# Laying out pixels for the values' stationaries in a small buffer, in a vision tower on one core

## The chip, the cores and the metric

The kernel runs on one core of one Trainium2 chip. The metric is the device time of one execution in microseconds; of several executions the median is taken.

## The reference

The input `x` is 128 images of 64 channels, 64 x 64 pixels, float32. Per image:

```python
x = features.reshape(b, c, h, s, w, s)              # windows of 4 x 4 pixels, s = 4
reduce_feats = x.mean((3, 5))...                    # one token per window: 256 tokens
unf = ...                                           # the 16 pixels of each window
q = _ln(reduce_feats) @ Wq.T                        # one query per window
kv = _ln(unf) @ Wkv.T                               # keys and values of 16 pixels
attn = softmax(einsum('bhpd,bhpnd->bhpn', q * scale, k))
aggre = einsum('bhpn,bhpnd->bhpd', attn, v)         # 8 heads
h = reduce_feats + aggre @ proj_w.T + proj_b
h = layernorm(h + lightning_attention(h))           # causal, with decay, chunks of 128
h = layernorm(h + moe(h))                           # 8 experts, top 2, gelu
```

The change concerns the values of the 16 pixels, `v`.

## The kernel before

Two blocks follow each other. The first (tokenizer and attention) works on 128 units; the second (experts) begins when it is done. A unit is one half (128 windows) of two images: 64 channels of one image lie on partitions 0 to 63, those of the other on 64 to 127, and the unit's 2048 pixels lie along the free dimension of one of the four buffers of `xb`. They stand in the order of the image: four pixel rows `b` of a window (512 floats each), in each the 128 windows `t`, in each window the four pixel columns `d`. SyncE loads a unit by four transfers (line 286) as soon as the unit four before has done its values (`v_pe`).

All engines run their own `step(i, r)`, written out by hand: unit 4i + r enters, and work on the units one to six before is interleaved with it, counted by semaphores. The steps of a loop iteration are four (r = 0 to 3); in every second one (s = 1) the attention's state is updated as well.

TensorE's order in a step is: `selected` (lines 317, 320: reduces keys and centred squares of the unit before), `attended` (455), `state` (462, s = 1), `keys(0)`, `attn_qk` (391, 392), `turned` (331, 332), `scores(0)` (412), `values(0)`, `keys(1)`, `attn_vk` (399), `values(1)`, `attend(0)` (427), `queries` (377), `keys(2)`, `scores(1)`, `values(2)`, `queries_turned` (385), `keys(3)`, `aggregated` (443), `values(3)`, `projected` (448), `attend(1)` (427, and 434 for s = 1). `keys_free(j)` ahead of `keys(j)` waits until VectorE and ScalarE have read the keys' two banks of the group before (`kq_done`, `cs_done`).

`keys(j)` (342, 347) multiplies the weights as stationary by the pixels of row j. `values(j)` (366) is the other way round: the pixels are the stationary, so that the windows come out on partitions. For pixel column j it takes, of each pixel row b, the pixels of 128 windows, which is every fourth float of `xb`, as one 128x128 stationary, and streams 128 columns of weights. Each fp32 product is issued as two passes, each with a weight load and a matmul; a group `values(j)` has 4 products and 8 passes. The result goes to the bank `VB`, and ScalarE copies it to `vs` (line 524).

ScalarE further squares the centred pixels (517), copies `oT` (529), `ssb` (533), `qT` and `kT` (542, 543), `vpad`, `vpl`, `kpl` and `htok` (555 to 563), takes over the queries (`qps`, 568), and begins the layer norms' inverse root (581 to 584). VectorE finishes it by a Newton step (818 to 820), scales the queries (825), forms key times query (`kqs`, 752), the softmax (835 to 858), the masks of the attention scores (763) and the reduction of values times weights (`agg`, 800). GpSimd multiplies values by weights (636, 643), and sums the pixels of the unit two ahead (666 to 674).

Of the kernel before, what the change touches and what calls it, by code (L numbers as in the profile page):

```python
# [6 lines left out]
ACT = mybir.ActivationFunctionType  # L7
# [6 lines left out]
def vit_tower_kernel(nc, x, ln_q_w, ln_q_b, Wq, ln_kv_w, ln_kv_b, Wkv, proj_w, proj_b,  # L14
                     w_qkv, w_proj, b_proj, slopes, router_w, w1, b1, w2, b2, out):
    P = 128
    B, C, HH, WW = x.shape
    ST = 4
# [17 lines left out]
    def done(i, r, lag, per, plus=0):  # L36

        if isinstance(i, int):
            return max(0, max(0, min(UNITS, 4 * i + r - lag + 1)) * per + plus)
        return i * (4 * per) + (r - lag + 1) * per + plus  # L40

    def there(i, r, lag):
        return not isinstance(i, int) or 0 <= 4 * i + r - lag < UNITS
# [20 lines left out]
    def units(eng, step):  # L64

        step(-1, 2)
        step(-1, 3)
        for i in (0, 1):
            for r in range(4):
                step(i, r)  # L70
        with eng.Fori(2, UNITS // 4 - 1) as i:
            for r in range(4):
                step(i, r)
        for u in range(UNITS - 4, UNITS + 6):
            step(u // 4, u % 4)

    with ExitStack() as ctx:
        def sb(name, shape, dt=F32):
            return ctx.enter_context(nc.sbuf_tensor(name, shape, dt))

        def sem(name):
            return ctx.enter_context(nc.semaphore(name))
# [6 lines left out]
        VB = ps[:, 2, :]  # L89
# [13 lines left out]
        w_ckv = sb("w_ckv", [P, 3 * P])  # L103
# [17 lines left out]
        with ExitStack() as early:  # L121
            def sb1(name, shape, dt=F32):
                return early.enter_context(nc.sbuf_tensor(name, shape, dt))
# [18 lines left out]

            xb = sb1("xb", [P, 4, PX])
            xt = sb1("xt", [P, PX // 2])
            l2 = sb1("l2", [P, P])
            vs = sb1("vs", [P, 2, N * P])
            kqs = sb1("kqs", [P, ST, PX // ST])
# [47 lines left out]
            x_in = [sem("x_in%d" % r) for r in range(4)]  # L195
            kc_pe = sem("kc_pe")
            kq_done = sem("kq_done")
            cs_done = sem("cs_done")
            v_pe = sem("v_pe")
            vs_done = sem("vs_done")  # L200
            sel_pe = sem("sel_pe")
# [49 lines left out]
            NL = ST  # L251
# [44 lines left out]
            def _(pe):  # L296
# [8 lines left out]
                def step(i, r):  # L305
# [54 lines left out]
                    def values(j):  # L360

                        if there(i, r, 0):
                            pe.wait_ge(vs_done, done(i, r, 1, ST, j))
                            xv = xb[:, r, :].rearrange("p (b t d) -> p b d t", b=ST, d=ST)
                            for b in range(ST):
                                mm = nc.tensor.matmul(VB[:, b * P:(b + 1) * P], xv[:, b, j], w_ckv[:, P:2 * P],  # L366
                                                      start=True, stop=True)
                            mm.then_inc(v_pe, 1)

                    def queries():  # L370
# [101 lines left out]
                    scores(0)  # L472
                    keys_free(1)
                    values(0)
                    keys(1)
                    attn_vk()
                    values(1)
                    attend(0)
                    keys_free(2)
                    queries()  # L480
                    keys(2)
                    scores(1)
                    values(2)
                    keys_free(3)
                    queries_turned()
# [8 lines left out]
            def _(act):  # L494
# [9 lines left out]
                def step(i, r):  # L504
# [3 lines left out]
                    def squares(src, dst, to=None):  # L508

                        return nc.scalar.activation(src if to is None else to, src, ACT.Square, accum_out=dst)  # L510

                    def centred(j):

                        if there(i, r, 0):
                            act.wait_ge(kc_pe, done(i, r, 1, ST, j + 1))
                            act.wait_ge(sel_pe, done(i, r, 1, 1))
                            nc.scalar.activation(sqs[:, j, :], CB, ACT.Square).then_inc(cs_done, 1)  # L517

                    def values(j):

                        if there(i, r, 0):
                            act.wait_ge(v_pe, done(i, r, 1, ST, j + 1))
                            act.wait_ge(pv_ch, done(i, r, 2, ST, j + 1 - ST))
                            nc.scalar.activation(vs[:, s, j * 4 * P:(j + 1) * 4 * P], VB, ACT.Copy).then_inc(vs_done, 1)  # L524

                    if there(i, r, 5):
                        act.wait_ge(o_done, done(i, r, 5, 1))
                        act.wait_ge(pr_done, done(i, r, 6, 1))
                        nc.scalar.activation(oT[:], B7[:, 0:P], ACT.Copy).then_inc(oT_done, 1)
# [14 lines left out]
                    if there(i, r, 5):  # L544
# [3 lines left out]
                            ins = squares(lt[:, m * C:(m + 1) * C], ssq[:, m:m + 1], l2[:, m * C:(m + 1) * C])  # L548
                        ins.then_inc(ln_sq, 1)
                    values(0)  # L550
                    centred(1)
                    if there(i, r, 3):
                        act.wait_ge(vk_pe, done(i, r, 3, 1))
# [8 lines left out]
                            nc.scalar.activation(kpl[:], B6[:, P:2 * P], ACT.Copy).then_inc(st_ev, 1)  # L562
                        nc.scalar.activation(htok[:, o, :], B6[:, 2 * P:3 * P], ACT.Copy).then_inc(vk_ev, 1)  # L563
                    values(1)
                    if there(i, r, -1):
                        act.wait_ge(qp_pe, done(i, r, -1, 1))
                        act.wait_ge(tq_pe, done(i, r, 0, 1))
                        nc.scalar.activation(qps[:], B6[:, 0:P], ACT.Copy)
                        for m in range(2):
                            ins = squares(B6[:, P + m * C:P + (m + 1) * C], ssq[:, 2 + m:3 + m], l2[:, m * C:(m + 1) * C])  # L570
                        ins.then_inc(qp_ev, 1)

                        nc.scalar.activation(h1[:, bass.ds(4 * i + r + 1, 1), :], red[:].unsqueeze(1),
                                             ACT.Copy, scale=1.0 / N).then_inc(rcp_done, 1)
# [22 lines left out]
                    if there(i, r, 1):  # L597
                        act.wait_ge(s3_done, done(i, r, 1, 1))
                        nc.scalar.activation(sgr[:, :, 0:SL], sgr[:, :, 0:SL], ACT.Exp,
                                             scale=TOK_SCALE / WS).then_inc(ex_done, 1)  # L600
                    values(3)
                units(act, step)

            @block.gpsimd
# [739 lines left out]
```

## Time and profile before

| | |
|---|---|
| median of 3 runs | 3491.15 us (3491.13 to 3492.43) |
| the profiled execution | 3490.56 us |
| its span | 3488.5 us |
| TensorE matmul busy | 3308.4 us, 95% |
| TensorE weight load busy | 2063.2 us, 59% |
| VectorE busy | 2025.1 us, 58% |
| ScalarE busy | 1488.5 us, 43% |
| GpSimd busy | 1746.6 us, 50% |
| mean granted clock of TensorE | 0.967 |

Weight loads and matmuls overlap. Ends of matmuls are modelled, so starts are the surer numbers: the distance from a group's start to the start of the next is what the group takes. The clock is given as a share of 2.4 GHz; 0.50 is 1.2 GHz. "Idle before" with an arrow names what ended an idle time; "issue" is time in which the engine waited for nothing that the profile shows.

### The profile page before, as it was taken

Reading aid. Unit: us, or ns where it says so; the run is one execution under the profiler, and the core shown is the slowest. Engines: PE = TensorE matmul, PEld = TensorE weight load, DVE = VectorE, ACT = ScalarE, POOL = GpSimd, SP = SyncE. Lnnn points to the kernel's source line nnn. Section 1 sums busy time; section 2 is a strip of 40 time slices with the busy share of each in tenths; the row PEclk is TensorE's granted clock in tenths of the full one; section 3 lists DMA queues with packets and bytes.
Section 4 is the critical chain, followed back from the end, with each engine's and each line's share of the span. In section 5 each row is a group of like instructions: output and inputs, shape, how many; then the busy total and the mean of one; then the engine's idle time right before and its main releaser. Section 6 shows DMA issues by size and latency. Waiting matters only on the chain. (4 is left out here: it accounts for less than half of the span.)

```text
span 3488.5 us, 68919 instructions
## 1 busy us (share of the span) xinstructions
PE 3308.4 (95%) x21221; PEld 2063.2 (59%) x21221; DVE 2025.1 (58%) x4349; ACT 1488.5 (43%) x4493; POOL 1746.6 (50%) x1789
## 2 busy tenths in 40 slices
PE   4999999999999999999999999999999976399998
PEld 2666666666666666666666666666666646244333
DVE  3566666666666666666666666666666650655554
ACT  2444444444444444444444444444444433244443
POOL 2655555555555555555555555555555530011211
PEclk9999999999999999999999999999999975599999
DMA  3322222222222222222222222222222100000000
GB/s 65 61 50 49 48 48 48 48 48 48 48 48 48 48 48 48 48 48 48 48 48 48 48 48 48 48 48 48 48 48 48 25 1 5 0 19 18 18 21 21
DMA packets 573517, 144.09 MB, mean 41 GB/s; under 512 B 573472, under 2 KB 573472, under 8 KB 573472
## 3 DMA queue, kind: packets, MB, share of 16 engines
q1 hardware_dynamic: 573472, 143.51, 21.3%
q8 instruction: 25, 0.41, 0.1%
q14 instruction: 20, 0.16, 0.0%
HBM read 135.08 MB, written 8.39 MB: 41 GB/s over the span
## 5 line engine op out<-in xcount | busy, mean ns | idle before, releaser
L366 PEld LDWEIGHTS ps<-w_ckv,xb 128*128 128x128 f32 x4096 | 1008.2, 327 | 218.1 <-issue 192.1
L366 PE MATMUL ps<-w_ckv,xb 128*128 128x128 f32 x4096 | 1048.1, 399 | 0.9 <-DVE kqs L752 0.8
L636 POOL TENSOR_TENSOR pv<-vs,aw 128x512 f32<-128x512 f32 x512 | 534.7, 1077 | 668.5 <-DVE aw L854 365.8
L524 ACT ACTIVATE vs<-ps 128x512 f32<-128x512 f32 x512 | 305.7, 597 | 848.8 <-PE ps L366 848.8
L342 PE MATMUL ps<-xb,w_ckv 64*64 64x512 f32 x2048 | 553.4, 617 | 0.0
L347 PE MATMUL ps<-xb,w_ckv 64*64 64x512 f32 x2048 | 553.3, 617 | 0.0
L752 DVE TENSOR_TENSOR kqs<-ps,qqT 128x512 f32<-128x512 f32 x512 | 350.9, 685 | 332.9 <-PE ps L347 332.9
L763 DVE TENSOR_TENSOR sm<-ps,decay 128x512 f32<-128x512 f32 x512 | 328.7, 683 | 155.2 <-PE ps L412 155.2
L517 ACT ACTIVATE sqs<-ps 128x512 f32<-128x512 f32 x512 | 304.7, 595 | 211.8 <-PE ps L347 211.8
L666 POOL TENSOR_TENSOR xt<-xb 128x512 f32<-128x512 f32 x256 | 325.3, 1292 | 20.3 <-issue 19.9
L643 POOL TENSOR_TENSOR pv<-pv 128x512 f32<-128x512 f32 x256 | 323.1, 1284 | 0.0
L412 PE MATMUL ps<-qm,kT 32*128 32x512 f32 x1024 | 292.3, 647 | 0.0
L427 PE MATMUL ps<-sm,vpad 128*32 128x128 f32 x4096 | 278.0, 279 | 9.5 <-DVE sm L763 9.5
L656 POOL TENSOR_TENSOR htok<-htok,bp_row 128x128 f32<-128x128 f32 x128 | 58.3, 456 | 424.0 <-ACT htok L563 424.0
L1287 DVE TENSOR_TENSOR hid<-ps,hid 128x512 f32<-128x512 f32 x256 | 162.5, 685 | 156.2 <-PE ps L1080 150.4
L800 DVE TENSOR_REDUCE agg<-pv 128x128 f32<-128x1024 f32 x128 | 248.2, 1939 | 0.6 <-POOL pv L643 0.6
L427 PEld LDWEIGHTS ps<-sm,vpad 128*32 128x32 f32 x4096 | 207.8, 111 | 47.4 <-DVE sm L763 10.1
L1187 ACT ACTIVATE hid<-ps,b1p 128x1024 f32<-128x1024 f32 x128 | 142.5, 1114 | 195.8 <-PE ps L1069 195.8
L782 DVE TENSOR_TENSOR lt<-ps,htok 128x128 f32<-128x128 f32 x128 | 37.3, 291 | 272.0 <-PE ps L462 136.7
L818 DVE SCALAR_TENSOR_TENSOR ps<-ps,y0s 128x48 f32<-128x48 f32 x136 | 29.4, 216 | 275.6 <-ACT y0s L584 275.6
L977 POOL TENSOR_TENSOR y<-y 128x512 f32<-128x512 f32 x32 | 33.2, 1039 | 268.2 <-ACT y L1200 268.2
L669 POOL TENSOR_TENSOR xt<-xt 128x512 f32<-128x512 f32 x128 | 162.2, 1267 | 10.0
(222 smaller groups left out, 4899.9 us busy)
## 6 DMA issues: line engine op xcount, KB each, us to landing
xb<-in_x_dram SPq DMA_DIRECT2D x512, 256.0 KB, 4.3
out_dram<-outb SPq DMA_DIRECT2D x128, 64.0 KB, 1.6
w1p<-in_L_ffn_w_dram SPq DMA_DIRECT2D x16, 16.0 KB
b2v<-in_L_ffn_b_dram SPq DMA_DIRECT2D x16, 2.0 KB
w2p<-in_L_ffn_w_dram SPq DMA_DIRECT2D x8, 16.0 KB
b1p<-in_L_ffn_b_dram SPq DMA_DIRECT2D x8, 0.2 KB
sm<-in_L_tok_Wkv_dram SPq DMA_DIRECT2D x4, 16.0 KB, 2.0
w_avki<-in_L_attn_w_qkv_dram SPq DMA_DIRECT2D x4, 16.0 KB, 2.8
```

The costliest lines, as they stand in the source:

```text
L342: nc.tensor.matmul(KB[own, :], w_ckv[own, 2 * P + m * C:2 * P + (m + 1) * C], xv[own, j], start=True, stop=True)
L347: mm = nc.tensor.matmul(CB[(1 - m) * C:(2 - m) * C, :], w_ckv[own, m * C:(m + 1) * C], xv[own, j], start=True, stop=True)
L366: mm = nc.tensor.matmul(VB[:, b * P:(b + 1) * P], xv[:, b, j], w_ckv[:, P:2 * P], start=True, stop=True)
L412: nc.tensor.matmul(SCB[g % 2], kT[hp, s, :], qm[hp, s, :], start=True, stop=True).then_inc(sc_done, 1)
L427: mm = nc.tensor.matmul(B7[g * W:(g + 1) * W, 0:P], vpad[:, s, at:at + W], sm[:, (4 * g + jj) * P:(4 * g + jj + 1) * P], start=(jj == 0), ...
L517: nc.scalar.activation(sqs[:, j, :], CB, ACT.Square).then_inc(cs_done, 1)
L524: nc.scalar.activation(vs[:, s, j * 4 * P:(j + 1) * 4 * P], VB, ACT.Copy).then_inc(vs_done, 1)
L636: nc.gpsimd.tensor_tensor(pv[:, at].rearrange("p (k d) -> p k d", d=D), vs[:, s, at].rearrange("p (k d) -> p k d", d=D), aw[:, j * W4:(j + ...
L643: nc.gpsimd.tensor_tensor(pv[:, j * 4 * P:(j + 1) * 4 * P], pv[:, j * 4 * P:(j + 1) * 4 * P], pv[:, (j + 2) * 4 * P:(j + 3) * 4 * P], ALU. ...
L666: ins = nc.gpsimd.tensor_tensor(xt[:, h * H:(h + 1) * H], xb[:, f, h * H:(h + 1) * H], xb[:, f, (h + 2) * H:(h + 3) * H], ALU.add)
L752: V.tensor_tensor(kqs[:, j, :].rearrange("p (t d) -> p t d", d=ST), KB.rearrange("p (t d) -> p t d", d=ST), qqT[:, s, :].unsqueeze(2).to_b ...
L763: V.tensor_tensor(sm[:, g * 512:(g + 1) * 512].rearrange("p (h c) -> p h c", c=P), SCB[g % 2].rearrange("p (h c) -> p h c", c=P), decay[:, ...
```

## The change

A buffer `xd` of two pieces, 128 x 512 floats each, is added. ScalarE gets a function `gather(j, ahead)`: it copies, for pixel column j, the 512 pixels of a unit (every fourth float of `xb`, four rows b of 128 windows t) to the piece j % 2 of `xd`, where they lie side by side, and counts `xd_done`. In ScalarE's step gather(2) follows the copy of values(0), gather(3) that of values(1), and gather(0) and gather(1) of the next unit follow the copy of values(3). Each waits until the values' group that used this piece last is done (`v_pe`); gather(0) also waits for the load of the unit. `values(j)` on TensorE waits for `xd_done` and takes its stationaries from `xd`. Products, their number and their order are the same.

```diff
+            xd = sb1("xd", [P, 2, 4 * P])
+            xd_done = sem("xd_done")
@@ TensorE, values(j)
                             pe.wait_ge(vs_done, done(i, r, 1, ST, j))
-                            xv = xb[:, r, :].rearrange("p (b t d) -> p b d t", b=ST, d=ST)
+                            pe.wait_ge(xd_done, done(i, r, 1, ST, j + 1))
                             for b in range(ST):
-                                mm = nc.tensor.matmul(VB[:, b * P:(b + 1) * P], xv[:, b, j], w_ckv[:, P:2 * P],
-                                                      start=True, stop=True)
+                                mm = nc.tensor.matmul(VB[:, b * P:(b + 1) * P], xd[:, j % 2, b * P:(b + 1) * P],
+                                                      w_ckv[:, P:2 * P], start=True, stop=True)
@@ ScalarE
+                    def gather(j, ahead):
+
+                        if there(i, r, -ahead):
+                            f = (r + ahead) % 4
+                            if j == 0:
+                                act.wait_ge(x_in[f], 16 * NL * (i + 1 + (r + ahead) // 4))
+                            act.wait_ge(v_pe, done(i, r, 1 - ahead, ST, j - 1))
+                            nc.scalar.activation(
+                                xd[:, j % 2, :].rearrange("p (b t) -> p b t", b=ST),
+                                xb[:, f, :].rearrange("p (b t d) -> p d b t", b=ST, d=ST)[:, j],
+                                ACT.Copy).then_inc(xd_done, 1)
@@ ScalarE, step
                     values(0)
+                    gather(2, 0)
                     centred(1)
@@
                     values(1)
+                    gather(3, 0)
@@
                     values(3)
+                    gather(0, 1)
+                    gather(1, 1)
```

## Rows read from the trace of the kernel before

**Rows 1.** Busy time by stretch: window, length, PE, PEld, DVE, ACT, POOL, clock, DMA.

```profile
1000.00:1500.00 500.00, 500.00 (x3274) 323.61 (x3266) 307.20 (x656) 220.87 (x736) 297.93 (x299) 1.00 0.25 48
```

**Rows 2.** Weight loads of four lines, 500 to 2500 us: duration ns min/median/max, first and last start.

```profile
L366 PEld LDWEIGHTS ps<-w_ckv,xb x2944: 307/329/348, 500.5 to 2499.0; 128*128 128x128 f32 x197
...
L331 PEld LDWEIGHTS ps<-ident,ssb x368: 196/209/214, 517.1 to 2495.9; 128*128 128x128 f32 x184
...
L443 PEld LDWEIGHTS ps<-ident,aggn x92: 137/138/140, 509.6 to 2488.4; 128*128 128x128 f32 x92
...
L392 PEld LDWEIGHTS ps<-hT,w_avki x184: 192/192/192, 516.8 to 2495.4; 128*128 128x128 f32 x184
```

**Rows 3.** Start-up: timeline of matmuls (start, duration, idle before), and one stretch's clock.

```profile
65.87 0.48 PE L385 MATMUL ps<-ident,q 128*128 128x128 f32 x1 [1.81 <-DVE kqs L752]
66.28 1.12 PE L342 MATMUL ps<-xb,w_ckv 64*64 64x512 f32 x2
...
68.19 2.23 PE L366 MATMUL ps<-w_ckv,xb 128*128 128x128 f32 x8
...
70.00:72.00 2.00, 2.00 (x10) 0.53 (x13) 0.00 (x0) 0.60 (x1) 0.00 (x0) 0.52 0.11 25
```

**Rows 4.** Timeline of matmuls, steady stage: start, duration; x is the passes.

```profile
1534.04 0.74 PE L427 MATMUL ps<-sm,vpad 128*32 128x128 f32 x10
...
1538.74 0.39 PE L392 MATMUL ps<-hT,w_avki 128*128 128x128 f32 x2
1538.96 0.64 PE L331 MATMUL ps<-ident,ssb 128*128 128x128 f32 x4
...
1540.72 2.14 PE L366 MATMUL ps<-w_ckv,xb 128*128 128x128 f32 x8
1542.79 0.65 PE L342 MATMUL ps<-xb,w_ckv 64*64 64x512 f32 x2
...
1544.56 1.90 PE L366 MATMUL ps<-w_ckv,xb 128*128 128x128 f32 x8
1546.39 1.07 PE L427 MATMUL ps<-sm,vpad 128*32 128x128 f32 x16
1547.39 0.70 PE L377 MATMUL ps<-w_qc,red 128*128 128x256 f32 x2
...
1552.06 0.29 PE L385 MATMUL ps<-ident,q 128*128 128x128 f32 x1
...
1555.63 1.07 PE L427 MATMUL ps<-sm,vpad 128*32 128x128 f32 x16
```

**Rows 5.** Timeline of ScalarE in the same unit.

```profile
1542.97 0.60 ACT L524 ACTIVATE vs<-ps 128x512 f32<-128x512 f32 x1 [2.74 <-PE ps L366]
...
1546.57 0.60 ACT L524 ACTIVATE vs<-ps 128x512 f32<-128x512 f32 x1 [1.03 <-PE ps L366]
1548.12 0.28 ACT L568 ACTIVATE qps<-ps 128x128 f32<-128x128 f32 x1 [0.95 <-PE ps L377]
```

**Rows 6.** Timeline of VectorE in this unit and the one before.

```profile
1532.16 1.28 DVE L763 TENSOR_TENSOR sm<-ps,decay 128x512 f32<-128x512 f32 x2
...
1549.99 0.22 DVE L818 SCALAR_TENSOR_TENSOR ps<-ps,y0s 128x48 f32<-128x48 f32 x1 [1.25 <-ACT y0s L584]
...
1551.29 0.68 DVE L752 TENSOR_TENSOR kqs<-ps,qqT 128x512 f32<-128x512 f32 x1
...
1553.88 1.28 DVE L763 TENSOR_TENSOR sm<-ps,decay 128x512 f32<-128x512 f32 x2
```

**Rows 7.** Two reductions on VectorE: durations ns min/median/max.

```profile
L800 DVE TENSOR_REDUCE agg<-pv x128: 1919/1942/1951, 95.4 to 2836.5; 128x128 f32<-128x1024 f32 x128
...
L1262 DVE TENSOR_REDUCE r<-lg x1: 2286/2286/2286, 2998.1 to 2998.1; 128x256 f32<-128x2048 f32 x1
```

**Rows 8.** A shorter wait in the start-up, and the busy time by stretch around it.

```profile
84.39 0.33 PE L385 MATMUL ps<-ident,q 128*128 128x128 f32 x1 [0.79 <-DVE kqs L752]
...
84.00:88.00 4.00, 3.61 (x21) 2.45 (x25) 3.47 (x10) 1.64 (x5) 0.79 (x1) 1.00 0.00 0
```

## The prediction

> **What bounds the kernel now.** I read the busy table by stretches first. In the long middle stage TensorE is busy without a gap at a granted clock of 1.00, that is 2.4 GHz, while VectorE is busy 61% of the time, GpSimd 60% and ScalarE 44% [rows 1]. So the order written out in `step` for TensorE sets the pace of a unit. The stretch from 500 to 2500 us holds 2944 weight loads of line 366, which is 92 units of 32, so a unit takes 2000/92 = 21.74 us [rows 2]. The reader should next ask what these 32 loads cost. A load of line 366, whose stationary picks every fourth float of `xb`, takes 329 ns; the loads of line 392 have the same 128x128 shape and type with adjacent floats and take 192 ns [rows 2]. Transposes show the same step on a smaller base: 209 ns from the strided `ssb` (line 331), 138 ns from the adjacent floats of `aggn` (line 443) [rows 2]. A transpose issues one load where an ordinary fp32 product issues two, and the surplus of 137 ns against 71 ns is about two to one, as if an ordinary load read each element twice. A second sign is the clock. Early on there is a stretch at half clock (0.52), in which the keys' matmuls stretch from 0.65 to 1.12 us a pair, yet the eight passes of a values group take 2.23 us, against 2.13 to 2.14 us at full clock [rows 3, 4]. What paces that group is therefore not the array but the fetch of its stationaries.
>
> **The stationaries.** In the steady unit the values(0) group starts at 1540.72 and the keys after it at 1542.79, so it takes 2.07 us; values(1) starts at 1544.56, attend(0) at 1546.39, so it takes 1.83 us with its first load hidden behind the work ahead [rows 4]. Eight passes in about 1.95 us are 0.245 us each. What will a pass cost from adjacent floats? The nearest row is line 392, two passes with stationary and moving operand of exactly this shape: they start at 1538.74 and the transposes after them at 1538.96, so 0.11 us a pass [rows 4]. I take 0.11. From below, loads of adjacent floats cannot be hidden better than that, as matmul and load are then about equally long. From above I take 0.16 us, a quarter of the 0.64 us that the four transposes of line 331 take with their ends included [rows 4], for a case in which load and matmul overlap less well; that adds 16 x 0.05 = 0.8 us to the two groups that count below, or 100 us over 128 units. With 0.11, values(0) takes one exposed load and eight passes, 0.99 us, and saves 1.08; values(1) takes 0.88 and saves 0.95. By the same reckoning values(2) and values(3) save about 1.07 and 1.0. Without any wait that would be 4.1 us a unit.
>
> **Where values(2) and (3) run into a wait.** After `queries` (line 377, 1547.39) ScalarE takes the result at 1548.12 and makes its squares and rsqrt; VectorE's Newton step starts at 1549.99, its `kqs` product for keys(2) runs from 1551.29 to 1551.97, and TensorE goes on with line 385 at 1552.06 [rows 4, 5, 6]. TensorE arrives there only 0.09 us after the releaser. So when values(2), which lies just ahead, gets 1.07 us shorter, TensorE waits for `kq_done` in keys_free(3) instead, and what stands behind that wait (line 385, keys(3), line 443, values(3)) does not move. This gain is nothing, or at most 0.1 us. The next gate is attend(1), which waits for the last mask: VectorE runs on without a gap and ends line 763 at 1553.88 + 1.28 = 1555.16, while attend(1) starts at 1555.63 [rows 4, 6]. With 0.08 us for the semaphore it can start 0.39 us earlier, although values(3) is a whole microsecond shorter. In the unit before, the mask ends at 1532.16 + 1.28 = 1533.44 and attend(1) starts at 1534.04, which leaves 0.52 us [rows 4, 6]. The mean is 0.46 us. `selected` behind it also waits for keys(3)'s `kqs`, 0.6 us after the mask; attend(1) needs longer than that (16 passes, 0.9 us), so this adds nothing.
>
> **The gathers on ScalarE.** Four copies of 128x512 are added to each unit, 512 in all. The trace has no ScalarE read of strided SBUF. From below a gather costs what line 524 costs, 0.60 us [rows 5]; a copy more can bring no gain by itself. From above I take VectorE's `agg` reduction, which reads SBUF with a stride of 512 B: 1942 ns for 1024 elements or 1.90 ns each, against 2286 ns for 2048 adjacent ones or 1.12 ns each [rows 7]. At 1.90 ns an element plus ScalarE's fixed part (0.60 us less 512 times an assumed 0.83 ns, so 0.17 us) a gather is 1.14 us. I take 1.0, which is 0.60 us plus 512 times the difference of 0.78, since the engines differ in pace and the surplus is what the stride adds. Back-to-back copies overlap by about 0.1, so a gather moves its followers by 0.9 us.
>
> Is that hidden? On the path stand gather(2) and gather(3), both ahead of the copy of the queries, line 568. Now line 524 of values(0) starts at 1542.97 and line 568 at 1548.12, 5.15 us later [rows 5]; with values(1) 0.95 us shorter, 4.20 us are left. Between them ScalarE has line 524 twice (0.49 each net of overlap), keys(1)'s square (0.5) and the copies of line 555 to 563 (0.8 where the state is updated), 2.28 us together by the starts in the timeline. That leaves 1.92 us for two gathers, or 0.96 each: just enough at 0.9, and short by 0.16 us in every second unit at the upper bound, +10 us in all. Checked for gather(3) alone, line 524 to line 568 is 1.55 us [rows 5], and 0.49 + 0.9 fits. Two more gathers follow values(3). Queued behind them is the copy `oT` (line 529), for which attended() on TensorE waits; between values(3) and attended() lie attend(1) and selected(), some 3.2 us, and 0.49 + 2 x 0.9 + 0.28 = 2.6 us fit. The new wait on `xd_done` stands in values(j), with keys, attend and queries queued behind it; each gather is issued two groups ahead, so I cost it at nothing, covered by the groups between. If that cover went, each missing microsecond would be paid on TensorE. VectorE is idle for 1.25 us ahead of the Newton step [rows 6]; its work before that (`agg`, `kd`) hangs on keys(1), from which the Newton step is now 0.95 us less far, so it still fits, by 0.3 us. GpSimd and the loads are not moved: the loads wait for the same `v_pe` and have three units of lead.
>
> **The sum.** Per unit 1.08 + 0.95 + 0.46 = 2.49 us; the waits ahead of values(3) hold back the other 1.6. Times 128 units this is 318 us. The profiled execution took 3490.56 us, 2.06 more than its span; its time and the median of 3491.15 differ by 0.6 us, which I ignore. 3490.6 less 318 is 3173 us, a unit of 19.25 us. The attention drain and the second stage are untouched.
>
> **Weighed against the skill.** The row first: a stride of four floats costs line 366 137 ns a load [rows 2]. The Trainium skill (SBUF — State Buffer, the note on SBUF lines under "Door 1: The DMA port swizzle") speaks of 16-byte lines, of which each new one costs and two hits are needed to hide it, but also says that 4 fp32 is how far one can stride for free. Taken literally, the last half makes this change worthless; by it the time is 3491 us. The trace sides with the first half. The Trainium skill (ScalarE: Activation LUTs, "Step-by-step: what each stage is for") also gives 0.833 ns an element regardless of function; by it a gather is the lower bound above, and the sum stays the same because gathers are hidden either way.
>
> **Rivals.** First, the stride is not what makes these loads long (a conflict of `xb` reads with GpSimd would be another reason). Against it stand the second strided line and the constant pace at both clocks [rows 2, 3]; GpSimd reads `xb` during only one of four groups. Then nothing is saved, the gathers fit in the old gaps (5.15 us against 4.1), and the time stays 3491 us: 3%. Second, the gathers cost more than the upper bound. At 1.5 us moved each, the path to line 568 is late by 2 x 1.5 less 1.92 in state units and some 0.35 less in the others, 0.9 us a unit, giving about 3290 us, and up to the old time beyond that: 6%. Third, slower than before, by TensorE's clock. The new waits are about 1.0 us ahead of line 385 and 0.5 ahead of attend(1). In the early stretch a wait of 1.81 us for this same `kqs` was followed by matmuls at half clock for some 6 us, the clock being 0.52 still from 70 to 72, and a keys group took 1.91 us (66.28 to 68.19) [rows 3]. If this happened in each unit, keys(3) +0.9 (half of 1.91), values(3) +0.9, attend(1) +0.8 and the small ones between +0.4 make 3.0 us, more than the 2.49 gained: 3173 + 384 = 3557 us. It decides from a low stretch of about 5.5 us per unit on. Against it: the same wait at 0.79 us left the clock at 1.00 in the stretch around and after it [rows 8]. I give it 5%. Fourth, the VectorE chain binds less than I read, and more than 2.9 us a unit are gained, under 3125 us: 4%.
>
> **How the numbers follow.** The forecast case has 82%: 3173 us, up to 3275 with the pass at 0.16 us, and down to 3125 for small gains in the chain (0.4 us a unit). The second and fourth rival are also faster, and a fifth of the third if it strikes few units; a tenth of the second may end near the old time. What can be told from no change is about 0.2%, 7 us. Faster 0.93, within 0.03, slower 0.04. The range 3125 to 3275 leaves 18% outside.
>
> **What would show it.** Line 366's loads near 190 ns and its groups near 1.0 us; TensorE now idle ahead of line 385 by about 0.9 us and ahead of line 427 by about 0.5 us, released by VectorE; 512 new ScalarE copies of 0.6 to 1.14 us; line 377 to line 385 unchanged at 4.67 us; clock 1.00. The prediction is wrong if line 366 keeps 0.245 us a pass, if line 568 waits behind a gather, or if the clock row of the middle stage falls below 1.00.

## The result and the profile after

The changed kernel takes 3215.22 us (median of 4 runs, 3214.2 to 3215.95) against 3491.14 us before. The ratio is 0.921, with a 95% interval from 0.9194 to 0.9226, so 276 us are gained where 318 were forecast. Its profiled execution has a span of 3213.2 us.

The middle stage by stretches (window, length, then busy time of PE, PEld, DVE, ACT, POOL, then clock and DMA), and the loads and the gathers from 500 to 2500 us (ns min/median/max), which answer [rows 1] and [rows 2]:

```profile
1000.00:1500.00 500.00, 471.33 (x3642) 266.58 (x3634) 348.70 (x722) 348.61 (x927) 334.86 (x336) 1.00 0.29 54
```

```profile
L368 PEld LDWEIGHTS ps<-w_ckv,xd x3285: 186/192/246, 500.1 to 2499.9; 128*128 128x128 f32 x194
...
L535 ACT ACTIVATE xd<-xb x410: 1117/1136/1503, 499.3 to 2492.8; 128x512 f32<-128x512 f32 x137
```

The loads fell from 329 to 192 ns, which is exactly that of line 392 before. The clock stayed at 1.00. TensorE, which had no idle time in this stage, now has 29 us in 500. A gather takes 1.14 us, the upper bound of the prediction.

TensorE's timeline over one unit and the ends of its neighbours (start, duration, in brackets the idle time before and its releaser), to be read beside [rows 4]:

```profile
1502.65 0.33 PE L387 MATMUL ps<-ident,q 128*128 128x128 f32 x1 [0.92 <-DVE kqs L770]
...
1512.53 1.16 PE L368 MATMUL ps<-w_ckv,xd 128*128 128x128 f32 x8
1513.62 0.65 PE L344 MATMUL ps<-xb,w_ckv 64*64 64x512 f32 x2
...
1515.38 1.05 PE L368 MATMUL ps<-w_ckv,xd 128*128 128x128 f32 x8
1516.37 1.07 PE L429 MATMUL ps<-sm,vpad 128*32 128x128 f32 x16
1517.37 0.70 PE L379 MATMUL ps<-w_qc,red 128*128 128x256 f32 x2
...
1521.78 0.33 PE L387 MATMUL ps<-ident,q 128*128 128x128 f32 x1 [0.55 <-DVE kqs L770]
...
1524.97 1.07 PE L429 MATMUL ps<-sm,vpad 128*32 128x128 f32 x16 [0.38 <-DVE sm L781]
...
1536.83 0.70 PE L379 MATMUL ps<-w_qc,red 128*128 128x256 f32 x2
...
1544.88 0.30 PE L429 MATMUL ps<-sm,vpad 128*32 128x128 f32 x2 [0.38 <-DVE sm L781]
```

A values group takes 1.09 us (1512.53 to 1513.62) or 0.99 us (1515.38 to 1516.37), where it took 2.07 and 1.83. From one `queries` to the next (1517.37 to 1536.83) are 19.46 us. And both waits that the prediction named are there: VectorE's `kqs` ahead of line 387, the masks ahead of line 429. ScalarE in the same unit, with the copy of the queries that the gathers might have delayed, answers [rows 5]:

```profile
1516.47 0.60 ACT L526 ACTIVATE vs<-ps 128x512 f32<-128x512 f32 x1
1516.97 1.15 ACT L535 ACTIVATE xd<-xb 128x512 f32<-128x512 f32 x1
1518.10 0.28 ACT L584 ACTIVATE qps<-ps 128x128 f32<-128x128 f32 x1
```

The copy starts 0.73 us after `queries`, as it did before (1547.39 to 1548.12 in [rows 4] and [rows 5]). The gathers fill the gap to the last tenth and delay nothing there.

### The profile page after: what moved, and what is told of

Same layout as the page of the kernel before. It is cut to its first block and busy times, and to the rows that moved or that the text cites. A ratio compares the mean times of both kernels' runs of the same rounds, so it can differ in the third digit from the quotient of the medians.

```text
span 3213.2 us, 69810 instructions
## 1 busy us (share of the span) xinstructions
PE 2883.6 (90%) x21221; PEld 1598.9 (50%) x21221; DVE 2061.8 (64%) x4349; ACT 2001.7 (62%) x5005; POOL 1751.3 (55%) x1789
## 5 line engine op out<-in xcount | busy, mean ns | idle before, releaser
L368 PEld LDWEIGHTS ps<-w_ckv,xd 128*128 128x128 f32 x4096 | 516.7, 194 | 233.0 <-issue 194.6
L535 ACT ACTIVATE xd<-xb 128x512 f32<-128x512 f32 x512 | 586.3, 1171 | 0.0
L368 PE MATMUL ps<-w_ckv,xd 128*128 128x128 f32 x4096 | 570.6, 283 | 1.1 <-ACT sqs L519 1.1
L429 PEld LDWEIGHTS ps<-sm,vpad 128*32 128x32 f32 x4096 | 208.6, 111 | 102.1 <-DVE sm L781 79.8
```

Source lines behind the costliest of these rows:

```text
L368: mm = nc.tensor.matmul(VB[:, b * P:(b + 1) * P], xd[:, j % 2, b * P:(b + 1) * P], w_ckv[:, P:2 * P], start=True, stop=True)
L429: mm = nc.tensor.matmul(B7[g * W:(g + 1) * W, 0:P], vpad[:, s, at:at + W], sm[:, (4 * g + jj) * P:(4 * g + jj + 1) * P], start=(jj == 0), ...
L535: nc.scalar.activation(xd[:, j % 2, :].rearrange("p (b t) -> p b t", b=ST), xb[:, f, :].rearrange("p (b t d) -> p d b t", b=ST, d=ST)[:, j ...
```

## Experiments

All comparisons are with the kernel before on the same chip. Where a run is set beside the changed kernel, chips can differ; the kernel before took 3490.1 to 3491.2 us in all of them. All diffs are against the changed kernel.

### Stride without gathers, gathers without the stride (e1, e2)

```diff
 e1: all gathers and the wait on xd_done are left out
-  nc.tensor.matmul(VB[...], xd[:, j % 2, b * P:(b + 1) * P], w_ckv[:, P:2 * P], ...)
+  nc.tensor.matmul(VB[...], xb[:, r, (4 * b + j) * P:(4 * b + j + 1) * P], w_ckv[:, P:2 * P], ...)
 e2: gathers and waits stay
-  nc.tensor.matmul(VB[...], xd[:, j % 2, b * P:(b + 1) * P], w_ckv[:, P:2 * P], ...)
+  nc.tensor.matmul(VB[...], xv[:, b, j], w_ckv[:, P:2 * P], ...)      # xv as before
```

> This kernel leaves out the gathers and takes the stationaries as adjacent floats straight from xb, so values are formed from the wrong pixels; all else is as in the changed kernel. Theory A (gathers are hidden; stride alone makes the loads long): weight loads 192 ns, 0.125 us a pass, unit 19.5 us, 3205 to 3220 us. Theory B (two gathers ahead of the queries' copy hold the path up by some 0.25 us a unit, which is part of the shortfall against the forecast): about 3185 us.

Measured: 3216.84 us, ratio 0.9215 (0.920 to 0.923), the same as with gathers. Its loads are from `xb` itself and take 192 ns. So adjacency is all that shortens the loads; reading `xb` while GpSimd and SyncE use it does not lengthen them. Theory B fell: the gathers do not hold up the steady units. The equal times are a sum of small differences, though. Without gathers a steady unit takes 19.61 us where the changed kernel has 19.52 (TensorE waits 88 us instead of 80 for `kqs` between 500 and 2500 us; see e9 below), the start-up is some 7 us shorter, and the part behind the last load 3.5 us. So the gathers cost nothing in the steady stage and a few microseconds in the start-up.

> Gathers and their waits are kept, but the stationaries come strided from xb as before. Theory A: loads 329 ns, gathers fit into ScalarE's old gaps, 3491 us within 5. Theory B (the buffer's other effects bring the gain): near 3215 us. Theory C (gathers cost by themselves, through the path or through SBUF): 3510 us or more.

Measured: 3518.22 us, ratio 1.0077 (1.0061 to 1.0094): 28 us more than before. Theory B (effects of the buffer) is out, theory A was off, and theory C right by its number. The path it runs through shows in TensorE's timeline of two neighbouring units, at line 458, which needs ScalarE's copy `oT`:

```profile
1511.93 0.46 PE L458 MATMUL ps<-w_ap,oT 128*128 128x128 f32 x2 [0.20 <-ACT oT L544]
1534.03 0.49 PE L458 MATMUL ps<-w_ap,oT 128*128 128x128 f32 x2
```

In the units in which it has less time, `oT` stands behind two gathers of 1.14 us and comes late. That became theory F, tested by e10 and e11 below. A steady unit takes 21.91 us here and 21.74 before, which makes 21 of the 28 us.

### What stride costs (e3, e9)

```diff
 e3: no gathers; stationaries of values(0..3) straight from xb
+  xb[:, r, b*512:b*512+128]                                                # stride 1
+  xb[:, r, b*512:b*512+256].rearrange("p (t d) -> p d t", d=2)[:, 0]       # 2; likewise 3 and 4
 e9: gathers kept, their source read with stride 1, 2, 3, 4 for j = 0..3
+  nc.scalar.activation(out_, x4[:, :, 0:128], ACT.Copy)                    # and so on
```

> No gathers; the four values groups take stationaries from xb with strides of 1, 2, 3 and 4 floats (wrong pixels for all but one offset). Theory A1 (a fetch brings 16 bytes and costs when it is new): loads of 192 ns for 1, the same for 2, about 260 ns for 3, 329 ns for 4. Theory A2 (whatever is not adjacent is slow): 192 ns for 1, 329 ns for 2, 3 and 4. Time near 3260 us, as values(0) and values(1) are fast.

Measured, loads at strides of 1, 2, 3 and 4 floats (ns min/median/max), in that order:

```profile
L368 PEld LDWEIGHTS ps<-w_ckv,xb x800: 186/192/192, 503.5 to 2488.7; 128*128 128x128 f32 x160
...
L371 PEld LDWEIGHTS ps<-w_ckv,xb x800: 196/196/197, 506.1 to 2491.5; 128*128 128x128 f32 x160
...
L374 PEld LDWEIGHTS ps<-w_ckv,xb x800: 251/261/261, 511.1 to 2496.7; 128*128 128x128 f32 x160
...
L377 PEld LDWEIGHTS ps<-w_ckv,xb x798: 329/329/347, 514.5 to 2499.9; 128*128 128x128 f32 x200
```

192, 196, 261 and 329 ns are what theory A1 named: at two floats to 16 bytes (64 pieces for 128 floats) a load costs nearly nothing more, and the 32 further pieces of stride 3, and again of stride 4, cost 65 to 68 ns. Up to a stride of 4 floats the pieces touched and the length covered grow together, so that it is pieces of 16 bytes that count is not shown by this. The time, one run, is 3273 us (3260 expected); the 13 us were not followed up.

> The changed kernel, with the four gathers reading xb at strides of 1, 2, 3 and 4 floats, each in a line of its own (wrong pixels for most). If ScalarE pays for each new 16 bytes at the rate of its stride-4 copy, (1.135 - 0.17) / 512 = 1.9 ns, the copies take 0.60, 0.65, 0.89 and 1.13 us; if any stride is slow, 0.60 and three times 1.13. Time about 3215 us in either case, as gathers are hidden there.

Measured, the gathers at strides 1, 2, 3 and 4:

```profile
L538 ACT ACTIVATE xd<-xb x102: 621/622/623, 511.9 to 2493.4; 128x512 f32<-128x512 f32 x102
L540 ACT ACTIVATE xd<-xb x102: 662/677/702, 512.4 to 2493.9; 128x512 f32<-128x512 f32 x102
```

```profile
L542 ACT ACTIVATE xd<-xb x102: 882/891/902, 500.9 to 2482.6; 128x512 f32<-128x512 f32 x102
L544 ACT ACTIVATE xd<-xb x102: 1130/1140/1149, 503.7 to 2485.3; 128x512 f32<-128x512 f32 x102
```

0.62, 0.68, 0.89 and 1.14 us: ScalarE shows the same curve. So the copy pays for stride 4 as well; it pays once and off the path, where TensorE paid twice (two passes) on it. The single time, 3226 us, is 11 above the changed kernel and above the 3215 expected, although its copies are shorter. The waits of TensorE from 500 to 2500 us (total us, times, longest) show where they are, e9 first, then the changed kernel:

```profile
PE ps L387 <- DVE kqs L776: 89.3, 102, 1.0
...
PE ps L387 <- DVE kqs L770: 79.8, 103, 1.1
```

That is 0.10 us more in each unit, 13 us over 128. VectorE's scaling of the queries, which stands ahead of this `kqs`, takes 0.72 us on the mean in e9 (0.71 in e1) and 0.62 in the changed kernel; what lengthens it is told below, in the part on the prediction.

### Which groups bring the gain (e5, e6)

```diff
 e5: values(0), values(1) from xd; no gather(2), gather(3)
+  if j < 2: pe.wait_ge(xd_done, done(i, r, 1, 2, j + 1))
+  xd[:, j, b * P:(b + 1) * P] if j < 2 else xv[:, b, j]
 e6: values(2), values(3) from xd; no gather(0), gather(1)
+  if j >= 2: pe.wait_ge(xd_done, done(i, r, 1, 2, j - 1))
+  xd[:, j - 2, b * P:(b + 1) * P] if j >= 2 else xv[:, b, j]
```

> Only values(0) and values(1) take their stationaries from the buffer (two gathers a unit, ahead by one unit); values(2) and values(3) read xb strided as before. Theory A (the last two groups stand ahead of waits for VectorE, so their gain is mostly lost): 1.82 us a unit are kept, 3258 us, and TensorE waits for neither line 387 nor the masks. Theory D (each group brings a like share of the 276 us): 3353 us.

Measured: 3281.5 us, ratio 0.9407 (0.9391 to 0.9423): 209 us gained, 23 short of theory A's 3258 us. TensorE has one wait from 500 to 2500 us, and it is that of e2 (total us, times, longest):

```profile
PE ps L459 <- ACT oT L545: 11.3, 50, 0.3
```

> The counterpart: only values(2) and values(3) take them from the buffer. Theory A: 0.41 us a unit, what the two gates gave in the changed kernel, 3439 us, with waits of 0.5 to 1.0 us ahead of the transposed queries. Theory D: 3353 us.

Measured: 3429.0 us, ratio 0.9828 (0.9812 to 0.9844): 61 us gained, where theory A had 52. Together 270 of the 276 us, split 3.4 to 1, although all four groups became shorter by about a microsecond. Theory D, an equal split, fell. In e6 the rest is seen as waits of TensorE (total us from 500 to 2500, times, longest):

```profile
PE ps L389 <- DVE kqs L770: 60.1, 95, 0.7
...
PE ps L431 <- DVE sm L781: 36.0, 94, 0.4
```

That is 1.0 us in each of 95 units.

### Taking the waits away (e4, e7, e8)

```diff
 e4, TensorE
-  attend(0); keys_free(2); queries()
+  keys_free(2); queries(); attend(0)
 e4, ScalarE: gather(3, 0) from behind values(1) to ahead of centred(2)
 e7, VectorE
   keys(2)
+  mask(2); mask(3)
   ... softmax steps, h1 ...
-  mask(2); mask(3)
   keys(3)
 e7, ScalarE
-  gather(1, 1)            # end of the step
+  gather(1, 0)            # ahead of values(0) of the next
 e8: all of these
```

> The changed kernel with queries() ahead of attend(0) on TensorE and gather(3) moved behind the root chain on ScalarE. Theory A (from the queries on, the chain over ScalarE and VectorE to kqs(2) holds TensorE up, 0.9 and 0.5 us of waiting a unit): attend(0) fills the wait ahead of line 387, the wait ahead of attend(1) shrinks to at most 0.4 us, 0.7 to 1.0 us a unit saved, 3090 to 3130 us. Theory D (the order of TensorE is not what counts, another engine's cycle sets the unit): 3215 us.

Measured: 3159.84 us, ratio 0.9051 (0.9036 to 0.9066): 55 us less than the changed kernel, so the wait was real and order matters (theory D fell), but the gain is short of 85 to 125. TensorE's wait, the step of VectorE ahead of it, and GpSimd beside that:

```profile
1509.70 0.33 PE L387 MATMUL ps<-ident,q 128*128 128x128 f32 x1 [0.28 <-DVE kqs L770]
```

```profile
1507.98 1.07 DVE L843 TENSOR_SCALAR q<-qps,yrs 128x64 f32<-128x64 f32 x2
```

```profile
1507.56 1.28 POOL L687 TENSOR_TENSOR xt<-xt 128x512 f32<-128x512 f32 x1
```

The wait went from 0.92 to 0.28 us, not to nothing: the scaling of the queries, two instructions, took 1.07 us here instead of 0.42. It also left the wait for the masks as it was, at 0.38 us, and it brought a new one ahead of the queries, for a copy of ScalarE (total us, times, longest, from 500 to 2500 us):

```profile
PE ps L379 <- ACT htok L578: 10.3, 51, 0.3
```

The waits for `kqs` fell from 79.8 to 30.9 us in this window, or by 0.47 us a unit; less the 0.10 of the new one that is the 0.37 us by which a steady unit became shorter (19.52 to 19.15), 48 of the 55 us.

> The changed kernel, with VectorE's mask(2) and mask(3) ahead of the softmax steps, and ScalarE's gather(1) moved from the end of the step to its idle time ahead of values(0) of the next. Theory A: attend(1) no longer waits 0.38 us for the masks; the next gate, the last kqs for selected(), is 0.35 us behind in one unit of two, so 0.35 us a unit, about 3172 us. Theory E (the gate ahead of line 387 gives everything, what follows has slack): 3215 us.

Measured: 3165.98 us, ratio 0.9072 (0.9057 to 0.9087): 49 us gained over the changed kernel, 43 expected. The wait for the masks is gone, and the next gate is the one named, at half the units (total us, times, longest):

```profile
PEld ps L319 <- DVE kqs L770: 12.9, 52, 0.3
```

> e4 and e7 together: queries() ahead of attend(0), gather(3) behind the root chain, masks ahead of the softmax, gather(1) moved. Theory A: the two gains add, 3160 less 43, about 3117 us. Theory E: no better than e4, 3160 us.

Measured: 3113.70 us, ratio 0.8922 (0.8907 to 0.8937). The two gains of 55 and 49 us add up almost fully, to 102. This version beats both kernels: 376 us under the kernel before, 102 under the changed one. In e4, e7 and e8 alike some 3.5 us of the gain lie behind the last load of a values group, in a part that no edit touched (675.7 us in the changed kernel, about 672 in the three). In a stretch of 100 us TensorE is busy for 98 again:

```profile
600.00:700.00 100.00, 98.09 (x773) 54.67 (x765) 72.29 (x156) 70.66 (x186) 67.63 (x68) 1.00 0.30 59
```

### The copy behind two gathers (e10, e11)

```diff
 e10: e2, and e11: e5, each with
-  gather(1, 1)            # end of the step
+  gather(1, 0)            # ahead of values(0) of the next
```

> As e2 (gathers kept, stationaries strided from xb), but gather(1) stands in ScalarE's idle time ahead of values(0) of the next step and no longer ahead of the copy oT. Theory F (the 28 us of e2 come from oT standing behind two gathers while attended() waits): back to 3491 us within 5. Theory G (the cost is in SBUF or in the copy of the queries): 3518 us as e2.

Measured: 3495.34 us, ratio 1.0016 (1.0006 to 1.0025); the ten runs lie between 3491.3 and 3501.8. Of e2's 28 us, 24 are gone, and no wait for `oT` is left. Theory F holds, but the 24 are not all its own. A steady unit went from 21.91 to 21.78 us, which is 17 us over 128 units, and the last load of a values group from 2843.6 to 2827.2. The rest came from behind that load, where the edit changes nothing (window, length, busy times, clock; e2, then e10):

```profile
2843.60:3517.10 673.50, 546.56 (x3287) 278.11 (x3286) 317.94 (x685) 260.60 (x422) 103.12 (x124) 0.84 0.06 13
```

```profile
2827.20:3491.70 664.50, 539.52 (x3287) 275.00 (x3286) 317.45 (x685) 260.45 (x422) 102.96 (x124) 0.85 0.06 14
```

With e10 this part took 9 us less than with e2 or the kernel before (673.3), at a slightly higher granted clock. What e10 keeps above the kernel before in the first part, 12 us up to the last load, is 0.03 us a unit and some 8 us in the first 20 units. In those, from 50 to 150 us, the granted clock was 0.90 with e2 and e10 and 0.97 before.

> As e5 (only values(0) and values(1) from the buffer), with gather(1) moved as in e10. Theory F: the 23 us that e5 lies above its expected 3258 us go, 3255 to 3262 us. Theory G: 3281 us as e5.

Measured: 3269.21 us, ratio 0.936 (0.9344 to 0.9376), above the 3255 to 3262 of theory F. Half of the 23 us went, and no wait for `oT` is left. Up to the last load the gain is 16 us (2613.5 to 2597.5), 0.13 us a unit as in e10; the part behind took 6 us more than in e5 (666.1 and 672.2). Where the others are, the list of waits says (total us, times, longest):

```profile
PEld ps L389 <- DVE kqs L770: 8.6, 50, 0.2
```

8.6 us in 2000 are 11 us over the stage: in every second unit VectorE's chain ends 0.17 us too late for the transposed queries, even with values(2) at full length. The prediction had TensorE arrive there 0.09 us after the releaser; that margin is not in all units.

## Why the prediction came out as it did

The direction, the mechanism and the range held; the size was 13% off (276 us against 318).

**The stationaries.** Right in kind: stride alone (e1, e3), 329 to 192 ns. The price of a pass was right too. What was mis-sized is the group: each of the two took 0.10 us more than forecast, 1.09 instead of 0.99 us and 0.99 instead of 0.88. The last pass of values(1), before and after, shows why:

```profile
1546.06 0.40 PE L366 MATMUL ps<-w_ckv,xb 128*128 128x128 f32 x1
```

```profile
1516.16 0.28 PE L368 MATMUL ps<-w_ckv,xd 128*128 128x128 f32 x1
```

After, eight passes start between 1515.38 and 1516.16, so 0.11 us apart, the very figure of line 392. But from the last pass to the first of `attend` (1516.37) there are 0.21 us. Before, these were 0.33 us (1546.06 to 1546.39), where passes started 0.23 us apart. The change to the smaller stationaries of `attend` or `keys` costs some 0.09 us more than a pass, before as after; behind values(3), where line 450's of 128x128 follow, it is missing (eight passes in 0.90 us, 1523.22 to 1524.12). The prediction counted it in the 1.83 and 2.07 us of before and left it out of the 0.88 and 0.99 of after. (The expectation of e1, 0.125 us a pass, divided this change among the passes.) values(0) and values(1) therefore save 0.98 + 0.84 = 1.82 us and not 2.03; 0.21 us times 128 are 27 us, the largest piece of the shortfall.

**The wait ahead of line 387.** Right: what stands behind it hardly moved, and TensorE now idles there for 0.55 to 1.02 us (once 1.09). From `queries` to line 387 the forecast had 4.67 us unchanged; it is 4.41 us in the unit shown (1517.37 to 1521.78), with the state update, and 4.8 in those without, 4.64 on the mean. e6 shows how little the last two groups give alone, e4 that filling the wait gives more.

**The wait for the masks.** The mean was right, 0.41 us against 0.46, the parts were not. In the unit shown with the state update, attend(1) starts 7.60 us after `queries` (1517.37 to 1524.97) instead of 8.24, which is 0.64 and not 0.39 earlier. In the other it is 8.05 (1536.83 to 1544.88) instead of 8.23. VectorE's scaling of the queries decides it, and its length goes with what GpSimd does beside it:

```profile
1501.14 0.65 POOL L689 TENSOR_TENSOR xt<-xt 128x256 f32<-128x256 f32 x1
```

```profile
1501.22 0.78 DVE L843 TENSOR_SCALAR q<-qps,yrs 128x64 f32<-128x64 f32 x2
```

```profile
1520.99 0.66 POOL L689 TENSOR_TENSOR xt<-xt 128x256 f32<-128x256 f32 x1
```

```profile
1520.71 0.42 DVE L843 TENSOR_SCALAR q<-qps,yrs 128x64 f32<-128x64 f32 x2
```

It takes 0.78 us where a GpSimd addition runs beside it and 0.42 where it falls into the gap between two. The first of its two instructions alone shows it:

```profile
1501.22 0.62 DVE L843 TENSOR_SCALAR q<-qps,yrs 128x64 f32<-128x64 f32 x1
```

It ends at 1501.84, GpSimd's addition at 1501.79. In e4 the first instruction begins at 1507.98 and lasts until 1508.88, and the addition beside it ends at 1508.84. In all 13 traces, from 500 to 2500 us, there are 759 such instructions that started 0.2 us or more before the end of a GpSimd instruction, and every one ended 0.05 to 0.06 us after it. The prediction shifted VectorE's chain as a rigid block. No run took GpSimd's work away; the evidence is that the end follows GpSimd's wherever the two fall.

**The gathers.** At 1.14 us they cost the upper bound and not 1.0, and were still hidden, by e1. Where the prediction checked `oT` ("2.6 us fit"), the number was too small: the copy of values(3), two gathers and `oT` are 0.49 + 2.2 + 0.27 = 2.96 us in e2, and up to 3.2 in the changed kernel. There it fits narrowly, in the units without state update:

```profile
1508.10 0.26 ACT L543 ACTIVATE oT<-ps 128x128 f32<-128x128 f32 x1
```

```profile
1508.56 0.49 PE L457 MATMUL ps<-w_ap,oT 128*128 128x128 f32 x2
```

`oT` is done 0.20 us before its use, hardly more than the 0.14 us that lie between the two in e2, where TensorE does wait for it, and attend(1) had been held up by 0.38 us for the masks, so without that wait the margin would be gone (an estimate from these rows). In e2, which has no such wait, the same gathers cost 21 us in the steady units. The step came out right for the kernel at hand, in part by luck, and was wrong in its margin.

**The sum.** A steady unit takes 19.52 us, from 103 of them, 2.23 less than before, where 2.49 were forecast: 0.21 for the change of line behind the two groups, 0.05 for the masks. Times 128 that is 285 us. Between the first and the last load of a values group, 127 units apart, lie 277.7 us less (2815.2 before, 2537.5 after, both from 54.4), so some 6 us are missing in the start-up, and from the last load to the end the kernel takes 2.4 us longer. The sum took every unit as steady. Together 27 us for the change of line, 6 for the masks, 6 in the start-up and 2 at the end are the 42 us that are missing. In the start-up the changed kernel waits longer than in any steady unit (TensorE's timeline), and the granted clock from 72 to 130 us is lower, 1.00 before and 0.94 after (the second and third fence):

```profile
98.88 0.33 PE L387 MATMUL ps<-ident,q 128*128 128x128 f32 x1 [2.59 <-DVE kqs L770]
...
116.41 0.33 PE L387 MATMUL ps<-ident,q 128*128 128x128 f32 x1 [2.20 <-DVE kqs L770]
```

```profile
72.00:130.00 58.00, 55.54 (x325) 35.74 (x321) 27.61 (x61) 26.57 (x76) 32.40 (x32) 1.00 0.37 73
```

```profile
72.00:130.00 58.00, 49.71 (x345) 26.88 (x339) 30.26 (x63) 41.24 (x95) 32.89 (x34) 0.94 0.36 72
```

**The rivals.** That stride is not the cause: excluded by e1 and e3. That the loads are long because GpSimd uses `xb` beside them: excluded by e1, whose loads read `xb` too. The literal rule of the Trainium skill (SBUF — State Buffer, "Door 1: The DMA port swizzle") that 4 fp32 can be strided for free is contradicted: it is 329 against 192 ns for loads and 1.14 against 0.62 us for copies. The other half of that note, two hits in a 16-byte line, agrees with e3 and e9: a stride of two floats costs a load 4 ns and a copy 0.06 us, and from three on both rise steeply. The Trainium skill's 0.833 ns an element on ScalarE (ScalarE: Activation LUTs, "Step-by-step: what each stage is for") is in keeping with the copy of 512 adjacent floats (0.62 us; no run varied the length) and not with a source at stride 3 or 4 (0.89 and 1.14 us). The clock rival did not strike in the steady stage: waits of 0.92 and 0.38 us in each unit left the granted clock at 1.00. It struck twice in the start-up: behind the waits of 2.59 and 2.20 us shown above the clock was 0.50, that is 1.2 GHz, from 99.7 to 103.1 and from 116.7 to 120.1 us. Before, only the stretch up to 72 us was low [rows 3], and the changed kernel has that one too.

## What to carry to other kernels

Where TensorE is busy all the time, look at how long its weight loads take for their shape; a stationary with a stride of 12 or 16 bytes, the two that were measured as slow, can be worth a copy on an engine that has time, and the copy pays the stride once. Count what a group takes from its start to the next group's, for the change to other stationaries at its end does not shrink with the passes. Then look for the next wait behind each shortened stretch: here the half of the shortened groups that stood ahead of waits for VectorE brought less than a quarter of the gain, and two changes of order, each with a gather moved, which computed nothing else, gave 102 us more. Ahead of a copy that another engine waits for, count what is queued with its measured length, and place new work in idle time further off, even if there is slack today.

## What was not expected of the hardware

The fetch of strided stationaries keeps its own pace: eight passes took 2.23 us at half clock and 2.13 at full [rows 3, 4], so this part of a kernel does not gain from the clock. With adjacent floats that is no longer so. A values group of the changed kernel at half clock:

```profile
68.32 2.07 PE L368 MATMUL ps<-w_ckv,xd 128*128 128x128 f32 x8
```

It takes 2.07 us, against 1.16 at full clock (1512.53 above): nearly all that the copy gains is lost while the clock is low. Loads and copies follow one curve by stride, nearly flat to two floats, steep from three. And a short VectorE instruction from SBUF varies with what GpSimd does beside it, between 0.42 and 1.15 us a pair, enough to decide which unit of two waits.
